# Four stacked cross attentions: the residual kept with its features on the partitions, and new order tables

## What is computed

```python
# layer 0
q, k, v = x @ Wq, ctx @ Wk, ctx @ Wv              # 1024 wide, 16 heads of 64
p = softmax(q k^T / 8 + col_bias)
x = x + (p v) @ Wo + bo
# layers 1, 2, 3
xn = x * rsqrt(mean(x * x) + eps) * norm_w
q, k, v = xn @ wq, ctx @ wk, ctx @ wv             # q 128 wide, k and v 32 wide
p = softmax(q k^T / sqrt(8))
x = x + (p v) @ wo
```

## Time and profile before

| | us |
|---|---|
| median of 3 runs | 1445.4 (1444.02 to 1445.58) |
| the profiled execution | span 1442.6 |
| PE busy | 1416.4 |
| PE weight loads | 1151.5 |
| DVE busy | 1090.9 |
| ACT busy | 1043.0 |
| POOL busy | 787.3 |

### The profile page before, as it was taken

The page is one execution under the profiler, slowest core; times in us unless marked ns, Lnnn a source line. Parts: engine busy times, 40 slices in busy tenths (PEclk is TensorE's granted clock), DMA queues, the critical chain, the costliest instruction groups (busy, mean ns, idle before and its releaser), DMA issues.

```text
span 1442.6 us, 56878 instructions
## 1 busy us (share of the span) xinstructions
PE 1416.4 (98%) x23692; PEld 1151.5 (80%) x23692; DVE 1090.9 (76%) x2281; ACT 1043.0 (72%) x2321; POOL 787.3 (55%) x905
## 2 busy tenths in 40 slices
PE   8999999999999999999999999999999999999987
PEld 6778878888888888788888788888888887888765
DVE  1557777777777777777778777777777777777887
ACT  3567776777777777767777777777777777677777
POOL 3445555545555455555455555455554555554687
PEclk9999999999999999999999999999999999999999
DMA  5010111010111001111001110101110001110000
GB/s 157 21 28 18 29 29 30 24 29 18 30 29 31 23 18 29 30 29 30 24 19 29 29 30 24 29 19 29 29 32 23 23 25 30 29 28 18 18 7 14
DMA packets 58540, 41.16 MB, mean 29 GB/s; under 512 B 17456, under 2 KB 54064, under 8 KB 58288
## 3 DMA queue, kind: packets, MB, share of 16 engines
q1 hardware_dynamic: 57872, 37.19, 9.9%
q10 hardware_dynamic: 416, 0.33, 0.1%
HBM read 20.68 MB, written 4.19 MB: 17 GB/s over the span
## 4 chain that ended last, share of the span: by engine, by line
PE 96%; ACT 1%; DVE 1%; POOL 1%; issue 1%; DMA 0%
PE bank L706 17%; PE bank L694 16%; PE bank L753 16%; PE bank L771 8%; PE bank L721 7%; PE scores L743 7%; PE bank L790 7%; PE scores L732 5%; PE bank L762 5%; PE bank L796 3%; PE bank L777 3%; PE bank L713 2%; PE bank L665 1%; ACT E L863 1%; DVE st L954 0%
## 5 line engine op out<-in xcount | busy, mean ns | idle before, releaser
L644 POOL TENSOR_TENSOR E<-E,st 128x512 f32<-128x512 f32 x512 | 530.2, 1044 | 535.7 <-DVE st L966 535.5
L963 DVE TENSOR_REDUCE st<-E 128x8 f32<-128x512 f32 x512 | 344.7, 675 | 81.0 <-ACT E L859 40.0
L863 ACT COPY E<-bank 128x512 f32<-128x512 f32 x512 | 298.1, 598 | 96.7 <-PE bank L753 95.5
L859 ACT ACTIVATE E<-E,inv 128x512 f32<-128x512 f32 x384 | 278.5, 734 | 57.2 <-DVE E L958 56.7
L954 DVE TENSOR_REDUCE st<-scores 128x8 f32<-128x512 f32 x372 | 244.0, 683 | 97.0 <-PE scores L743 97.0
L753 PE MATMUL bank<-ident,E 128*128 128x128 f32 x2048 | 301.5, 276 | 0.9 <-POOL E L644 0.7
L753 PEld LDWEIGHTS bank<-ident,E 128*128 128x128 f32 x2048 | 241.5, 141 | 69.3 <-issue 28.2
L706 PE MATMUL bank<-wv,cT 128*128 128x374 f32 (+1 forms) x768 | 271.4, 478 | 0.0
L694 PE MATMUL bank<-cT,wk 128*128 128x256 f32 x1024 | 245.9, 384 | 7.0 <-issue 5.9
L958 DVE TENSOR_TENSOR E<-scores,st 128x512 f32<-128x512 f32 x372 | 245.9, 669 | 0.1
L694 PEld LDWEIGHTS bank<-cT,wk 128*128 128x128 f32 x1024 | 188.9, 192 | 32.1 <-issue 6.3
(11 more groups left out here) (58 smaller groups left out, 1627.0 us busy)
## 6 DMA issues: line engine op xcount, KB each, us to landing
KB<-K SPq DMA_DIRECT2D x1536, 8.0 KB
cT<-in_ctx_t SPq DMA_DIRECT2D x32, 256.0 KB, 2.8
xq<-in_x_t SPq DMA_DIRECT2D x32, 128.0 KB, 2.2
xin<-in_x SPq DMA_DIRECT2D x32, 128.0 KB, 2.3
out<-xN SPq DMA_DIRECT2D x30, 128.0 KB, 1.9
wk<-in_L_xattn_Wk SPq DMA_DIRECT2D x3, 256.0 KB, 5.5
wv<-in_L_xattn_Wv SPq DMA_DIRECT2D x2, 374.0 KB, 6.4
wq<-in_L_xattn_Wq SPq DMA_DIRECT2D x1, 512.0 KB, 6.2
```

What stands on the lines that cost most here:

```text
L644: e.tensor_tensor(E3, E3, wide(stat[s][u][:, 16:24]), ALU.mult).then_inc(g_nrm.sem, 1)
L859: e.activation(E[s][u][:, :], E[s][u][:, :], ACT.Exp, scale=inv[s][:, u // 2:u // 2 + 1]).then_inc(a_exp.sem, 1)
L863: e.copy(E[s][u][:, :], bank_of["t", g, l, u][:, :]).then_inc(a_et.sem, 1)
L963: e.tensor_reduce(stat[s][u][:, 8:16], heads(E[s][u][:, :]), AX, ALU.add).then_inc(d_sum.sem, 1)
```

## The change

1. The residual is kept with its features on the partitions only, in `xT`. `wo0` and `wo` have the weights stationary and the attention output moving, 256 columns at once: 8 matmuls in place of 16 for `wo0`, one in place of two for `wo`. DVE adds the product, the bias (now one value per partition) and `xq` into `xT`; `xin`, `xN`, their loads and POOL's `xb` go. `q` reads `xT` as it lies. PE's transpose of the residual now feeds only the squares (`x2` is a PE step and an ACT step that reads PSUM), and ACT's copy `xt` goes. The input `x` is given only in transposed form and the output is stored transposed.
2. All order tables are new, with a period of 43.249725 in place of 43.53; there are no tables for the last groups.
3. `SPLIT` is empty: the last groups run like all others.
4. `PE_FILL` is zero.

```diff
-PE_FILL = (18, 18, 16, 16)
-PERIOD = 43.53
+PE_FILL = (0, 0, 0, 0)
+PERIOD = 43.249725
 PE_TIME = {
-    "k": {0: (30.28, 0, 14.31, 51.16)},
-    "v": {0: (21.14, 37.8, 49.25, 36.09, 39.27, 41.84)},
-    "k3": {0: (47.45,)},
...
+    "k": {0: (-21.58522, -64.80264, -64.71223, -21.51657)},
+    "v": {0: (-21.59932, -21.58321, -21.52759, -21.59361, -21.55707, -21.57032)},
+    "k3": {0: (-21.57964,)},
+    "q0": {0: (21.65369, 21.65068, 21.65158, 21.65191)},
+    "s": {0: (21.65862, 21.65929), 1: (23.65929,), 2: (65.00401,), 3: (108.17619,)},
+    "t": {0: (21.71338, 21.73215, 21.73978, 21.75232),
+          1: (64.91515, 64.93467, 64.91679, 64.94518),
+          2: (108.1535, 108.15655, 108.15601, 108.15763),
+          3: (108.25867, 108.26131, 108.2756, 108.26559)},
+    "pv0": {0: (21.75315, 21.75374)},
+    "wo0": {0: (21.76377,)},
+    "x2": {1: (21.81504,), 2: (64.98476,), 3: (108.17258,)},
+    "q": {1: (21.80292,), 2: (64.98359,), 3: (108.1664,)},
+    "pv": {1: (64.96913,), 2: (108.16345,), 3: (108.34216,)},
+    "wo": {1: (64.97639,), 2: (108.1648,), 3: (151.39963,)},
 }
...
-SPLIT = range(NG - 2, NG)
+SPLIT = range(NG, NG)
...
-        bo = sb("bo", [128, C])
+        bo = sb("bo", [128, 1])
...
-            for s in range(NS):
-                e.dma_start(xin[s][:, :, :], x_r[s]).then_inc(l_x[s].sem, 16)
...
                 elif kind == "lt" and g + NX < NG:
                     w.wait_ge(p_ev, *[("q0", g, 0, i) for i in range(4)])
+                    w.wait_ge(d_ev, *[("wo0", g, 0, part(g, p)) for p in range(NP)])
                     e.dma_start(xq[g % NX][:, :], t["x_t"][g + NX]).then_inc(l_xq[g % NX].sem, 16)
...
-                    for p in halves(g, u):
-                        for j in range(8):
-                            m = e.matmul(bank[:, 128 * p:128 * p + 128], QT[s][:, j, 128 * p:128 * p + 128],
-                                         wo0[:, j, :], start=(j == 0), stop=(j == 7))
+                    for j in range(8):
+                        m = e.matmul(bank[:, tokens], wo0[:, j, :], QT[s][:, j, tokens], start=(j == 0), stop=(j == 7))
                     m.then_inc(p_ev.sem, 1)
                 elif kind == "q":
-                    w.wait_ge(a_ev, ("xt", g, l, u))
+                    w.wait_ge(d_ev, ("wo0" if l == 1 else "wo", g, l - 1, u))
...
+                elif kind == "x2":
+                    w.wait_ge(l_ident, "ident")
                     w.wait_ge(d_ev, ("wo0" if l == 1 else "wo", g, l - 1, u))
                     for p in halves(g, u):
-                        to_rows(bank, 128 * p, xN[s][:, p, :], p == halves(g, u)[-1])
+                        m = e.transpose(bank[:, 128 * p:128 * p + 128], xT[s][:, 128 * p:128 * p + 128], ident[:, :])
+                    m.then_inc(p_ev.sem, 1)
...
-                    for p in halves(g, u):
-                        m = e.matmul(bank[:, 128 * p:128 * p + 128], QT[s][:, 1, 128 * p:128 * p + 128],
-                                     wos[:, l - 1, :], start=True, stop=True)
-                    m.then_inc(p_ev.sem, 1)
+                    m = e.matmul(bank[:, tokens], wos[:, l - 1, :], QT[s][:, 1, tokens], start=True, stop=True)
+                    m.then_inc(p_ev.sem, 1)
...
-                    e.tensor_tensor(flat(xN[s])[:, tokens], bank[:, tokens], flat(xin[s])[:, tokens], ALU.add
-                                    ).then_inc(d_ev.sem, 1)
+                    e.scalar_tensor_tensor(xT[s][:, tokens], bank[:, tokens], bo[:, 0:1], xq[g % NX][:, tokens], ALU.add,
+                                           ALU.add).then_inc(d_ev.sem, 1)
```

More of the change, by code:

```diff
@@ L73 @@
[L73 to L77, removed]
+    "k": {0: (-8.77921, -36.70678, -20.503, 10.94194)},
+    "v": {0: (-16.03604, -6.3508, 9.52089, -12.44568, -0.58981, -0.64582)},
+    "k3": {0: (-5.5991,)},
+    "q0": {0: (30.69802, 27.97146, 27.93575, 28.51184)},
+    "exp": {0: (34.64696, 42.54139, 49.49182, 42.24318),
+            1: (76.52634, 71.23204, 74.89336, 77.36236),
+            2: (107.00093, 107.2207, 107.384, 110.86855),
+            3: (138.00192, 139.20966, 140.3618, 135.34549)},
@@ L78 @@
+    "et": {0: (50.33247, 52.92603, 59.92182, 60.16537),
+           1: (78.14329, 89.53222, 85.20667, 86.0407),
+           2: (115.82357, 119.28471, 117.41203, 119.30089),
+           3: (149.78006, 150.19284, 152.32961, 150.99612)},
+    "pv0": {0: (62.25493, 62.43579)},
+    "x2": {1: (70.42294,), 2: (98.54622,), 3: (126.40018,)},
+    "q": {1: (66.47984,), 2: (97.61452,), 3: (121.8724,)},
+    "pv": {1: (94.72735,), 2: (120.85064,), 3: (154.23125,)},
 }
 DVE_TIME = {
-    "add": {0: (77.25, 81.06, 83.78, 79.49)},
@@ L81 @@
[L81 to L98, removed]
+    "add": {0: (35.51291, 38.57546, 43.00497, 41.96354)},
+    "max": {0: (35.87869, 43.04855, 45.46796, 42.83665),
+            1: (78.3399, 71.77171, 71.7424, 74.1734),
+            2: (101.23989, 101.81088, 103.52753, 108.56275),
+            3: (136.05153, 133.25635, 134.57108, 134.4895)},
@@ new lines @@
+    "sum": {0: (44.22577, 49.04699, 53.21462, 47.48126),
+            1: (79.9654, 78.72339, 78.73203, 85.4603),
+            2: (108.15546, 103.91891, 109.55125, 113.13518),
+            3: (141.58232, 142.97308, 144.35388, 139.65706)},
+    "rcp": {0: (47.87789, 51.11113, 53.42168, 54.49127),
+            1: (80.16922, 85.13686, 83.95788, 88.69496),
+            2: (112.00701, 106.81554, 112.58089, 114.83434),
+            3: (143.84514, 144.05495, 145.29291, 139.87038)},
+    "wo0": {0: (64.17776,)},
@@ L99 @@
+    "ssq": {1: (71.29745,), 2: (101.21854,), 3: (132.3624,)},
+    "sub": {1: (78.62495, 73.7417, 76.74013, 74.63273),
+            2: (102.95918, 102.96375, 103.90149, 108.74641),
+            3: (138.41231, 135.14854, 136.83736, 135.16547)},
+    "wo": {1: (97.83303,), 2: (128.74098,), 3: (159.91617,)},
 }
 POOL_TIME = {
[L101 to L106, removed]
@@ L191 @@
-    30: {
-        "q0": {0: (72.734, 70.98, 74.935, 70.11)},
-        "exp": {0: (84.612, 82.427, 88.584, 86.674),
[13 rows of a table removed]
[L207 to L212, removed]
-        "exp": {0: (74.028, 75.662, 78.804, 77.384),
[13 rows of a table removed]
-    },
 }
 DVE_ENDS = {
-    28: {
-        "max": {3: (174.243, 182.484, 178.047, 175.599)},
-        "sum": {3: (184.053, 185.015, 180.915, 180.237)},
-        "rcp": {3: (184.806, 185.974, 182.283, 183.162)},
-        "ssq": {3: (167.97,)},
-        "sub": {3: (181.593, 183.363, 179.136, 177.156)},
-        "wo": {2: (166.881,), 3: (192.458,)},
-    },
@@ L448, in xattn_kernel @@
         powers = sb("powers", [128, 2, NP])
-        xin = [sb(f"xin{s}", [128, NP, C]) for s in range(NS)]
         xq = [sb(f"xq{i}", [128, T]) for i in range(NX)]
-        xN = [sb(f"xN{s}", [128, NP, C]) for s in range(NS)]
         xT = [sb(f"xT{s}", [128, T]) for s in range(NS)]
@@ L520, in xattn_kernel @@
         l_b = signal("l_b", range(7), 16)
-        l_x = [signal(f"l_x{s}", range(s, NG, NS), 16) for s in range(NS)]
         l_xq = [signal(f"l_xq{i}", range(i, NG, NX), 16) for i in range(NX)]
@@ L591, in sync_program @@
                 s = g % NS
-                if kind == "xT" and g + NS < NG:
-                    w.wait_ge(d_ev, ("wo0", g, 0, 0))
-                    e.dma_start(xin[s][:, :, :], x_r[g + NS]).then_inc(l_x[s].sem, 16)
-                elif kind == "cT" and g + NC < NG:
+                tokens = slice(128 * halves(g, u)[0], 128 * halves(g, u)[-1] + 128)
+                if kind == "cT" and g + NC < NG:
                     w.wait_ge(p_ev, ("k3", g, 0, 0), *[("k", g, 0, i) for i in range(4)], *[("v", g, 0, i) for i in range(6)])
@@ L612, in sync_program @@
                     w.wait_ge(d_ev, ("wo", g, 3, u))
[L613 to L614 removed]
+                    e.dma_start(t["out"][g][:, tokens], xT[s][:, tokens]).then_inc(s_o[s].sem, 16)
             for g in range(NG - NS, NG):
@@ L631, in gpsimd_program @@
                 s = g % NS
-                if kind == "xb":
-                    w.wait_ge(l_x[s], g)
-                    e.tensor_tensor(xin[s][:, :, :], xin[s][:, :, :],
-                                    bo[:, :].rearrange("p (a c) -> p a c", a=1).to_broadcast([128, NP, C]), ALU.add
-                                    ).then_inc(g_xb.sem, 1)
-                elif kind == "sub":
+                if kind == "sub":
                     E3 = heads(E[s][u][:, :])
@@ L661, in tensor_program @@
             w = Engine(e)
-            def to_rows(bank, lo, src, st):
-                m = e.transpose(bank[:, lo:lo + 128], src, ident[:, :])
-                if st:
-                    m.then_inc(p_ev.sem, 1)
             for st in PE_ORDER:
```

257 lines of the change are left out of this document (30 added, 227 removed), and 55 rows, old and new, of tables (ACT_ENDS, PE_ENDS).

## The result

The changed kernel takes 1497.4 us (median of 3 runs, 1489.13 to 1500.61) against 1445.4: the ratio is 1.0354 [1.0320, 1.0387], so it is 3.5% slower. The forecast was 1459 in a range up to 1473: the direction was right, the size was not. The three runs of the changed kernel lie 11 us apart and those of the kernel before 2 us, so differences to the changed kernel are known to some 5 us by the medians; the starts of steps in the traces tell them more sharply. The profiled execution has a span of 1495.6 us, 53.0 more than before.

A forecast was written before the change was run, and what follows sets the result against it. PE's throughput was taken to bound only the middle stage. Middle 0, head +2.0, tail +8.7 and tail clock +3.0 gave +13.7 us: span 1456.3, plus 2.8 a median of 1459 us; own range 1450 to 1466, with rivals 1441 to 1473.

The forecast's parts named there:

- costs nothing in the middle: Middle: the `PE_FILL` waits, 68 a group, are met at once and cost nothing; removing 18 at the start gives -1.0 us.
- the middle period stays at 43.8: Middle: one group still takes 43.8 us, no change; bounds -0.2 to +0.5 us per group.
- The bound of +16 us for the middle: Middle: upper bound over 32 groups, +0.5 us per group if several narrow places in the new order open.
- Output weights stationary: `wo0` and `wo` on PE, every group: fewer, wider matmul records gain 0.17 us per group.
- the fifth cluster of small matmuls: Middle: the new order has five clusters of small tiles per period instead of four, +0.15 us per group.
- rival 2: Middle: ACT comes late at narrow places, 0.5 us per group, 16 us in all, giving 1475; chance 0.12.
- Head: Start of run: PE starts at about 4.9, 1.0 us earlier, then stalls 3.0 us at `k3`; +2.0 us in all.
- the clock for the tail: Tail: the lower clock slows PE's work on the path; 0 to about +8 us, taken as +3.
- The packed block: Tail: the last block still having `q0` and `s` of layer 0 (group 31) takes 36.9 us, PE working 28.5.
- the walk: Tail: steps followed from `s1` of group 31 to the end, 51.5 us; one unsplit layer alone takes 15.6 us.
- the tail of the kernel before, 29.6: End of the old kernel: cost beyond PE's own work, 41.0 us of head and tail less 11.4 for the head.
- Rival 1: Tail: lower clock from mid layer 1 on, +8 instead of +3, and packed block at its worst: 1466 to 1472; chance 0.12.

The follow-up runs named there:

- moved padding: Changed kernel plus 79 wait instructions per group (1536 instructions again), two each before the `v` and `k` that follow a `pv`, the rest elsewhere: 1472.3 us.
- the two phases of one padding: Changed kernel plus 79 waits per group, spread ahead of `k`, `v`, `k3`, `q0`: 1481.5 us; more left out in first groups, shifting the stream 113 instructions: 1546.0 us.
- the run with everything mended: Changed kernel with 79 waits per group at moved places, group 0's `k3` placed later, and added transposes in the last two groups: 1458.3 us.

## Why the prediction was wrong

- **`PE_FILL`, "costs nothing in the middle", is the step that failed**, with the sentence behind it that the middle period stays at 43.8. I priced the fills as work and found none, and never asked whether their number does something. Position in the stream was worth 25 us here (shown by moved padding against the changed kernel, and by the two phases of one padding), and removing the fills alone costs the kernel before 41 us. With position mended the kernel takes 1472.3, just within the range, and is still slower than before, so the direction wasn't luck. The bound of +16 us for the middle came from open places of ACT and POOL, so it couldn't hold this. The kernel before showed a hint: the page's instruction queue with its 192 packets, 6 for each of the 32 groups.
- **Output weights stationary: right.** 16 records take 3.46 us, forecast 3.44 (721.22 - 717.76 above). The gain of 0.17 us a group showed as 0.10 with the old tables and 0.14 with the new ones. No cost shows for the fifth cluster of small matmuls (+0.15 in the sum): with and without it the period is 43.7. The new order as such was neither a gain nor a loss in the middle, and no rival 2 showed: with 43.68 in every group nothing waits for ACT there.
- **Head: +3.8 instead of +2.0.** The start at 4.79 (4.9) and the wait at `k3` of 3.46 (3.0) were right. Missing was the clock behind the wait, about 3 us; I had summed the clock for the tail only. With it the sum would be -1.1 + 3.5 + 3.0 = +5.4, of which 3.8 are left at `wo0` of group 2; what takes 1.6 us back on the way there stays open (I had allowed the ramp of layers 1 us).
- **End: both terms too small.** By the cuts of the table it is +27.2. The packed block took 39.1 us from `s1` to `s1` (1392.64 to 1431.76), forecast 36.9, and the last full period 0.6 more than 43.8. From the last `s1` to the end it is 62.7 (1432.9 to 1495.6), forecast 51.5 + 3 for the clock, so 8.2 too little. Keeping the clock up gives back 6.7 (56.0 in the run with everything mended) where I had taken 3, and the walk was 4.5 short: a lone layer takes 18.0 us, not 15.6. So these two terms named the right mechanisms and were mis-sized. Last, the tail of the kernel before, 29.6, was a remainder of a sum: my own stretches, laid at these cuts, give 142.7 us behind `wo0` of group 29 for the changed kernel (a period of 43.8, the block of 36.9, 7.5 from `wo0` to the end of `s1`, 51.5 and 3), and 142.7 - 126.4 is +16.3, not the +11.7 of the sum. A difference of two cuts of the trace would have shown these 4.6 us.
- Rival 1, the cold tail, came true in the end. That its 1466 to 1472 is near the 1472.3 of the kernel with its phase mended is in part luck: head and walk have their share in that.

In sum, from 1497.4: position 25.1, clock and wait in head and tail 14.0, undivided end with its tables 16.9 (1458.3 - 1441.4; a remainder, in the profiled runs +17.3 for the end behind `wo0` of group 29, -2.5 for the head and -0.9 for the middle), which leaves 1441.4, the 3 to 4 us that the data flow gains. The forecast had +13.7 for head, tail and clock, where the runs give 14.0 + 16.9 = 30.9, and nothing for position.

## What to carry to other kernels

An instruction that does nothing can still have a job: where an engine runs through hundreds of short instructions without a pause, count its stream and see on which steps the block borders of the page's instruction queue fall, before and after an edit that changes the count. Waits marked "issue" in the middle of a group of small matmuls are the sign. A count per loop turn that is a multiple of a block makes their place the same every time, for good (1481.5 us here) or for bad (1546.0). Price a standstill of TensorE with the slower clock behind it, and judge an edit of the data flow and a new order in separate runs: here the first gained some 3 us and the rest hid it under 56.

## What the runs showed of the hardware

- PE's instructions come in packets of 16.4 KB, 256 of 64 bytes. Where the last three quarters of 256 instructions or all of them are small matmuls (2.0 us of work for all), the crossing costs up to 2.3 us, always at instruction 194 or 195 of a block (92 of 92 waits with starts over 0.7 us apart, in three kernels; that they aren't at 0 or 255 stays unexplained). PE goes on 1.2 to 1.6 us after the end of a packet. What within the loading takes the time is open; the packets themselves are mostly recorded with 0.9 to 1.4 us. The same crossing can cost 1.4 us in one execution and nothing in another.
- Wait instructions that are met at once are free behind long matmuls, and cost 0.2 us for five or six behind a `pv`.
- A standstill of 3.5 us at the head was followed by 7 us at a granted clock of 0.51, one of 2.1 us at the same step by none; and in the end, where PE stands between lone softmax layers, the clock is at 0.50 to 0.60 over the last 36 us; 60 added transposes in the longest standstill and 85 before it gave back 8.2 us.
